# TensorE's half-slot of a three-layer decoder: row-maximum tiles ahead of the score tiles, in place of behind them

## What is computed

```
x = layernorm(x + linear_attention(x))        # state = 0.99 state + 0.01 v k^T, read before it is updated
x = layernorm(x + cross_attention(x, ctx))    # 16 heads of 16, softmax over 512 keys
x = layernorm(x + self_attention(x) + moe(x)) # 16 heads of 16; top 2 of 8 experts, experts of 256 x 256
```

## Time and profile before

| | |
|---|---|
| time, median of 3 runs | 1357.91 us (1356.98 to 1358.36) |
| the profiled execution: its own time | 1358.7 us |
| its span (first to last instruction) | 1356.9 us |
| TensorE busy | 1251.6 us (92%) |
| VectorE busy | 903.9 us (67%) |
| ScalarE busy | 776.9 us (57%) |
| GpSimd busy | 364.8 us (27%) |
| mean granted TensorE clock | 0.966 |

### The profile page before, as it was taken

The page is one execution under the profiler, slowest core; times in us unless marked ns, Lnnn a source line. Parts: engine busy times, 40 slices in busy tenths (PEclk is TensorE's granted clock), DMA queues, the critical chain, the costliest instruction groups (busy, mean ns, idle before and its releaser), DMA issues.

```text
span 1356.9 us, 19260 instructions
## 1 busy us (share of the span) xinstructions
PE 1251.6 (92%) x6624; PEld 598.3 (44%) x6624; DVE 903.9 (67%) x1808; ACT 776.9 (57%) x1087; POOL 364.8 (27%) x435
## 2 busy tenths in 40 slices
PE   6789888999999999999999999999999999997995
PEld 3333344454444444444444544444444444443442
DVE  5367665566776767766777677767677677666672
ACT  2235554656657665656657565566556566564664
POOL 2300011321522225212243115222252123331162
PEclk9769988999999999999999999999999999998999
DMA  6804314134332144333223343431243333303300
GB/s 225 137 17 64 63 18 55 41 48 78 49 59 51 24 74 64 64 49 48 62 46 54 47 79 48 63 62 25 43 63 48 48 48 48 61 4 48 48 18 16
DMA packets 49840, 74.85 MB, mean 55 GB/s; under 512 B 8520, under 2 KB 20048, under 8 KB 49488
## 3 DMA queue, kind: packets, MB, share of 16 engines
q1 hardware_dynamic: 48736, 73.09, 33.1%
q10 hardware_dynamic: 1008, 0.53, 0.1%
HBM read 18.02 MB, written 4.19 MB: 16 GB/s over the span
## 4 chain that ended last, share of the span: by engine, by line
PE 77%; DVE 10%; issue 5%; ACT 4%; DMA 2%; SPq 1%; POOL 0%; DVEq 0%; ACTq 0%
PE ms L406 38%; PE sc L406 14%; PE op L406 14%; PE mx L406 7%; DVE maxes L808 4%; PE ms L425 2%; PE ms L480 2%; DVE k_parts L723 2%; ACT k_parts L600 1%; ACT probs L660 1%; DMA qs<-q_parts 1%; SPq L356 1%; DMA qs<-shift_r 1%; DVE x1b L764 1%; PE ms L475 1%
## 5 line engine op out<-in xcount | busy, mean ns | idle before, releaser
L808 DVE TENSOR_REDUCE maxes<-mx 128x1 f32<-128x512 f32 x1024 | 658.0, 684 | 362.4 <-PE mx L406 361.2
L660 ACT ACTIVATE probs<-sc 128x1024 f32<-128x1024 f32 x512 | 524.3, 1024 | 467.8 <-PE sc L406 463.3
L969 POOL TENSOR_TENSOR x<-x,moe 128x256 f32<-128x256 f32 x256 | 186.8, 730 | 643.6 <-ACT moe L653 618.6
L406 PE MATMUL op<-probs,v 128*32 128x512 f32 x2048 | 280.0, 619 | 2.2 <-ACT probs L660 1.1
L406 PE MATMUL sc<-qs,ks 50*128 50x512 f32 x1024 | 260.6, 506 | 11.1 <-ACT probs L660 7.7
L406 PEld LDWEIGHTS sc<-qs,ks 50*128 50x128 f32 x1024 | 96.9, 186 | 330.1 <-ACT probs L660 227.1
L406 PE MATMUL mx<-ks,qs 48*128 48x512 f32 x1024 | 211.9, 409 | 23.4 <-DVE maxes L808 15.3
L653 ACT ACTIVATE moe<-ms,comb 128x256 f32<-128x256 f32 x256 | 106.8, 472 | 17.6 <-PE ms L406 17.6
L406 PEld LDWEIGHTS mx<-ks,qs 48*128 48x128 f32 x1024 | 100.2, 192 | 31.5 <-DVE maxes L808 21.2
L406 PE MATMUL ms<-we_hi,x2T_hi 128*128 128x512 f32 x256 | 96.0, 456 | 6.3 <-DVE lin L742 3.5
L406 PEld LDWEIGHTS op<-probs,v 128*32 128x32 f32 x2048 | 40.9, 109 | 96.7 <-issue 94.8
(11 more groups left out here) (104 smaller groups left out, 1193.1 us busy)
## 6 DMA issues: line engine op xcount, KB each, us to landing
ks<-k_parts SPq DMA_DIRECT2D x192, 128.0 KB, 4.7
qs<-q_parts SPq DMA_DIRECT2D x192, 128.0 KB, 5.5
xT_s<-in_xT SPq DMA_DIRECT2D x8, 512.0 KB, 4.8
x_s<-in_x SPq DMA_DIRECT2D x8, 512.0 KB, 3.9
ctxT_s<-in_ctxT SPq DMA_DIRECT2D x8, 512.0 KB, 3.9
out<-x SPq DMA_DIRECT2D x7, 512.0 KB, 2.9
qs<-shift_r SPq DMA_DIRECT2D x128, 8.0 KB
probs<-in_we SPq DMA_DIRECT2D x1, 1024.0 KB, 7.7
```

The lines of the kernel that those rows point to most:

```text
L406: return nc.tensor.matmul(dst, lhsT, rhs, start=first, stop=last, skip_group_check=True)
L660: nc.scalar.activation(probs[:, (2 * s + h) % 3, :, :], sc[:], ACT.Exp).then_inc(exp_out, 1)
L808: nc.vector.tensor_reduce(maxes[:, g % 2, at:at + 1], mx[:, i % 3, :], AX_X, ALU.max).then_inc(max_out, 1)
L969: nc.gpsimd.tensor_tensor(x2[:, n % 2, t, :], x2[:, n % 2, t, :], moe[:, k % 2, j * D:j * D + D], ALU.add).then_inc(acc, 1)
```

## The change

On TensorE, `max_tiles` now stands ahead of `scores` in each half-slot where both run. `values` and the units stay behind both. No wait, buffer, count or instruction is added or taken away, and the orders of VectorE, ScalarE, GpSimd and SyncE are what they were.

```diff
@@ -580,10 +580,10 @@
                 if t == lin_at("kc0", 0):
                     pe.wait_ge(w_late, 16 * len(LATE))
                     pe.wait_ge(scaled, 4)
+                if 0 <= s + MAX_LEAD < SLOTS * len(PHASES):
+                    max_tiles(4 * (s + MAX_LEAD) + 2 * h)
                 if 0 <= s < SLOTS * len(PHASES):
                     scores(s, h)
-                if 0 <= s + MAX_LEAD < SLOTS * len(PHASES):
-                    max_tiles(4 * (s + MAX_LEAD) + 2 * h)
                 if h == 0 and 1 <= s <= SLOTS * len(PHASES):
                     if s == 1:
                         pe.wait_ge(fills, 5)
```

## The result

The changed kernel takes 1377.9 us (median of 4 runs, 1372.9 to 1379.0) against 1358.1: a ratio of 1.013, interval 1.011 to 1.015. In a second series the same kernel took 1373.4 us and the ratio was 1.010 (1.007 to 1.013, experiment `e4_again`). It is slower by 1.0 to 1.3%. The profiled execution took 1372.9 us, with a span of 1371.1; the three others of its series took 1377.6 to 1379.0, and no profile shows where their 5 us more are.

The account below looks back on a forecast made before the run. The prediction took TensorE's own stream plus its waits to bound the kernel. Its terms, 16.4 - 6.3 + 0.3 + 1.1 - 1.3 = +10.2 us, gave a median of 1368 us, forecast 1362 to 1374 (chance 0.66), range 1360 to 1379.

Parts of the forecast that it names:

- rival D: Behind the gate unit, longer stalls may bring more lower-clock stretches; one in each of seven batches adds 11 us, 1379; chance 0.10.
- The shifts: After each half's swapped pairs, the exponential starts 0.23 us later and the reductions 0.23 to 0.25 us earlier.
- Part 1, the stalls behind the exponential: TensorE's waits on k_parts, heads, x (L678) and q_parts each grow by 0.23 us: 39 places, 9.0 us.
- Part 1, the units whose data arrive just in time: At 25 units such as kc1, 0.10 us of cover lets 0.13 of the 0.23 come through: 3.2 us.
- The five `moe6` behind `q3c1`: These five units have 0.13 us of cover against the later exponential; they lose 0.5 us together.
- Part 2, the gains: Where VectorE takes units out without ScalarE, stalls behind the reductions shrink by 0.23 us: 27 places, -6.3 us.
- one of the signs by which the prediction would be wrong: In the profile after, the stretches at the lower clock multiply (rival D).
- Rival B: In some 250 slots the score pair's weight load finds no cover, costing 0.10 us each: 25 us, 1393; chance 0.07.
- Rival C: The low part waits for VectorE's reductions, not the high part, turning 39 places to -0.23: 1350 us; chance 0.05.
- Rival A: Across slots, the shifts cancel because a longer stall is taken off a later one: no change; chance 0.12.
- Part 3: Waits at the pairs themselves: +0.3 on maxes, +1.1 on stack DMAs, -1.3 on shift's DMA; score waits on the exponential unchanged.
- the DMA wait of the second stack: One of two waits for a stack's DMA, each forecast to cost 0.34 + 0.23 us, 1.1 together.

Follow-up runs that it names:

- e4_again: The changed kernel once more, nothing altered: 1373.4 us (1370.4 to 1374.2), ratio 1.010 against the kernel before.
- e3_select: Kernel before, with maximum tiles ahead of scores only in halves h = 0 that follow cy0, cy1, v3a or v1: 1359.3 us, 1.001.
- e5_slots: Kernel before, with maximum tiles first in both halves of the slots whose h = 0 follows cy0, cy1, v3a or v1: 1356.1 us, 0.997.
- e6_h1_slots: Kernel before, with maximum tiles first in every half h = 1, and in h = 0 only behind cy0, cy1, v3a or v1: 1359.3 us, 1.000.
- e9_best: Kernel before, maximum tiles first in both halves of slots behind cy0, cy1, v3a, and in h = 1 from t = 96 to 455: 1357.3 us, 0.997.
- e10_gate_twice: Kernel before, with the gate's sixteen matmuls of 8 columns issued twice in a row: 1377.9 us in its one execution.
- e7_fill_after: Changed kernel, with three wide matmuls put ahead of the gate's narrow ones: 1375.9 us, 1.013.
- e8_fill_before: Kernel before, with three wide matmuls put ahead of the gate's narrow ones: 1368.5 us, 1.008.

## Why the prediction was right where it was, and where it was off

The sign, the mechanism of the shifts and nearly all places were right; the time forecast was 1368 us, and 1373 to 1378 were measured. The first series' 1377.9 lies outside the 1362 to 1374 of the forecast itself and inside the stated range only by the room left for rival D, whose cause isn't borne out. The forecast's +10.2 stands against some 9 us that the traces give to the order up to the last stage; the other half of the +19.8 of the first series was not foreseen as such, and that the total still lay in the range is in part luck.

**The shifts.** Forecast were 0.44 from score to exponential and 0.53 from maximum to reduction; these are the numbers of the rows above. The steps are 0.23 to 0.25.

**Part 1, the stalls behind the exponential.** Right, at every place named: `k_parts`, `x`, `q_parts`, `heads` behind a low part. `x2T0` idles 0.82, forecast 0.8.

**Part 1, the units whose data arrive just in time.** This is the term that was mis-sized. The prediction gave 25 units 0.13 us each; the steps there are 0.24. Their start is late by what was forecast. The unit `kc1`:

```profile
783.74 0.29 PE L475 MATMUL ms<-w_ident,shift_n 128*32 128x128 f32 x1
...
784.00 0.30 PEld L406 LDWEIGHTS ms<-ctxT_s,w_wk 128*128 128x128 f32 x2 [0.17 <-ACT moe L653]
784.00 1.98 PE L406 MATMUL ms<-ctxT_s,w_wk 128*128 128x512 f32 x4
```

It stands 0.26 behind `shift`, 0.12 before (781.42 to 781.54), which is 0.14 more. But its four matmuls now take 1.98 us and took 1.88. The weight load used to go in under `shift`; now it waits for the `moe` take-out and is in the open. The cover of 0.10 that the prediction counted was the time of the weight load itself. That is 25 x 0.10 = 2.5 us more for the whole kernel. The five `moe6` behind `q3c1`, forecast at 0.1 each, show no step.

**Part 2, the gains.** Right: -0.23 to -0.24 at `cy1`, `moe13`, `s1`, `moe0`.

For a batch of the repeated part, the prediction's text has 158.3 us and the trace 158.58 (156.90 before). With the weight loads the account closes: 7 + 4 steps of 0.24, 0.07 at `moe8`, less 4 of 0.24, is 1.75, against 1.68 measured.

**Rival D, the clock.** Its price held, 1.6 us a stretch; its cause isn't shown. The batches with a lower clock were three in the first profile, one of the signs by which the prediction would be wrong, and one in the second. In both profiles of the changed kernel they come behind the gate, not behind the longest stalls. The one idle time shortly ahead that is new is 0.23 us (`q1` on `q_parts`, at 635.07). It isn't needed: `e3_select`, `e5_slots`, `e6_h1_slots` and `e9_best` have such stretches behind the gate with no idle of TensorE in the 7 us before. Some kernels have them behind the 1.2 us of waits at `moe0` as well, where the kernel before has none in its four batches. Whether the change makes them more frequent is open. In neither profile of the kernel before is there one within the four batches, but there is one just ahead of them and one behind, so of the six gates from 320 to 1130 two have one in both of its profiles, and four and two in those of the changed kernel. In the profiles of the kernels with another order, one to three batches of the repeated part had one. That is too few to tell. Also open is why the first series gave 1.3% and the second 1.0%.

**Rival B** is refuted: the second pair takes 0.40 us whichever it is, and its weight load starts 0.10 behind the first pair, under it (786.46 above). The page "TensorE: Matmul & The Clock Gate" of the Trainium skill, section "Step-by-step: what each phase is for", names two cases in which a load is pulled ahead: row groups that don't conflict, and a load into the background weight buffer. The prediction took up the first alone, so the 25 us don't follow from that section. Which case this load is, no run here shows. Nor does a first pair cost 0.43, as the prediction has it: from its start to that of the second it is 0.34 (783.79 to 784.13).

**Rival C**: the two arrivals, 0.08 us apart before, moved apart the way that was foreseen; VectorE's low part now waits 0.59 for ScalarE. **Rival A**: the stalls did not absorb each other, except where `heads` waited for `shift_r`: 0.06 there in place of 0.24.

**Part 3** was near in one term: at the DMA wait of the second stack the net step is +0.39, forecast 0.57. It was wrong in another: the waits of the score pairs on the exponential, which it left unchanged, fell from 7.7 us to 1.7, while the maximum pairs wait 4.5 us longer for `maxes`. In slots with few units, in the first and last batch, the wait has moved from the one pair to the other; the traces show no net gain from it (the first 94 half-slots cost 1.1 more). What the prediction did not see is how close the order stands to the exponential. It priced the margin at 0.05 and called it the same in either order, which is true only because both halves were turned round; turning h = 0 alone costs 3.4%.

## What to carry to other kernels

When two pieces of work swap places on the busiest engine, its own time stays, and each partner's start moves by the length of the other piece; count the places where TensorE already waits for each partner, and the difference is the price. Keep the order that serves the partner with more waits, and turn it round only at the places that wait for the other, having checked what then stands between two dependent pieces. A margin read as the gap from a take-out to a matmul may be a weight load and no margin.

## What the runs showed of the hardware that was not expected

- The first pair of half-height matmuls (48 or 50 rows) behind full-height work (128 rows) takes 0.50 us and the second 0.40, whichever tiles they are: 511 ns for the maximum and 406 for the score tiles after the change, 409 and 506 before. The second pair's weight load runs under the first pair (786.46 to 786.65, pair from 786.36).
- A weight load that has to wait for a semaphore moves into the open and adds 0.10 us to the matmuls behind it (1.88 to 1.98 us).
- The granted clock can fall to 0.50 behind a stretch of 8-column matmuls with no idle time of TensorE (650.20 in `e10_gate_twice`). With the stretch doubled to 3.7 us it fell there in four of five batches, in one execution. Three wide matmuls (some 0.7 us) ahead of it did not prevent it once (487.6 in `e7_fill_after`).
- It also falls some 12 us later, behind two waits of 0.56 and 0.69 us (653.30 in `e8_fill_before`). In which batches it falls changes from execution to execution of one kernel.
